# One fp32 chunk instead of three, x1's products and sum at other places, and one low part on VectorE

## What is computed

```python
e = jnp.stack([tbl_f[ids[:, f]] for f in range(39)], axis=1)      # 512 x 39 x 16
x0 = xk = e
for W in (f0, f1, f2):             # 39*39 x 128, 128*39 x 128, 128*39 x 128
    z = jnp.einsum('bfd,bgd->bfgd', x0, xk).reshape(b, f * g, d)
    xk = jnp.einsum('bpd,pm->bmd', z, W)
    outs.append(xk)
z = jnp.sum(jnp.concatenate(outs, axis=1), axis=-1)               # 512 x 384
h = jnp.concatenate([z, dense_ctx], axis=1)
h = jnp.maximum(h @ W_top1 + b_top1, 0.0)
h = jnp.maximum(h @ W_top2 + b_top2, 0.0)
y = h @ W_top3
```

## Time and profile before

| | before |
|---|---|
| median of 3 runs | 680.94 us (680.06 to 683.67) |
| profiled execution, its own time | 676.92 us |
| its span | 674.9 us |
| busy: PE, weight loads, DVE, ACT, POOL | 636.6, 504.6, 565.5, 374.1, 533.3 us |
| first bank of tiles 1, 2, 3, 4, 8 at | 83.9, 121.1, 158.4, 194.8, 348.3 us |
| last bank of the last tile ends at | 650.0 us |
| PE's granted clock | 0.995 of full speed |

### The profile page before, as it was taken

One profiled execution on the slowest core, in us unless ns is written; L12 is line 12 of the kernel. 1 busy time (PEld: TensorE's weight loads), 2 busy tenths in 40 slices (PEclk: granted clock), 3 DMA queues, 4 the chain that ended last, 5 costly groups with the idle time before them and its releaser, 6 DMA issues.

```text
span 674.9 us, 11454 instructions
## 1 busy us (share of the span) xinstructions
PE 636.6 (94%) x2900; PEld 504.6 (75%) x2900; DVE 565.5 (84%) x1934; ACT 374.1 (55%) x1129; POOL 533.3 (79%) x528
## 2 busy tenths in 40 slices
PE   3388999999999999999999999999999999999998
PEld 1256667777778788888878888888878888887867
DVE  4468888979899898989789898989879898988760
ACT  0445464646556574747467564746557474755431
POOL 6757879999999999998879999897969988574420
PEclk9999999999999999999999999999999999999989
DMA  9535642203241313113230322204031221200000
GB/s 185 112 70 140 211 117 68 62 6 89 40 110 18 98 29 81 44 29 95 43 85 8 84 44 66 60 10 113 10 88 37 63 62 41 81 0 1 2 0 1
DMA packets 79940, 42.25 MB, mean 63 GB/s; under 512 B 56721, under 2 KB 64721, under 8 KB 79746
## 3 DMA queue, kind: packets, MB, share of 16 engines
q1 hardware_dynamic: 67246, 35.85, 20.7%
q10 hardware_dynamic: 7380, 4.38, 3.2%
q0 software_dynamic: 5248, 1.29, 1.9%
HBM read 39.52 MB, written 1.94 MB: 61 GB/s over the span
## 4 chain that ended last, share of the span: by engine, by line
PE 68%; POOL 14%; DVE 5%; issue 5%; SPq 3%; ACT 2%; DMA 2%; POOLq 0%; DVEq 0%
PE y L900 16%; PE y L902 15%; PE y L901 15%; DVE scaled L802 4%; POOL emb_quads L481 4%; PE side L907 4%; PE late L918 4%; PE acc L882 3%; PE acc L877 3%; PE acc L876 3%; POOL sum L514 2%; POOL z_parts L499 2%; POOL sum L507 2%; ACT scaled L594 2%; PE y L918 2%
## 5 line engine op out<-in xcount | busy, mean ns | idle before, releaser
L802 DVE SCALAR_TENSOR_TENSOR scaled<-y,x_rows,scaled 128x128 f32<-128x128 f32 x1728 | 465.4, 341 | 63.4 <-ACT scaled L594 51.7
L594 ACT ACTIVATE scaled<-y,x_rows 128x128 f32<-128x128 f32 x768 | 218.9, 367 | 221.0 <-PE y L902 220.9
L900 PE MATMUL y<-w_hi,x_parts 128*128 128x512 f32 (+1 forms) x640 | 280.5, 438 | 9.5 <-DVE scaled L802 3.4
L902 PE MATMUL y<-w_hi,x_parts 128*128 128x512 f32 (+1 forms) x640 | 248.1, 388 | 0.0
L901 PE MATMUL y<-w_lo,x_parts 128*128 128x512 f32 (+1 forms) x640 | 247.6, 387 | 0.0
L481 POOL DMA_INDIRECT emb_quads<-in_small_tables_dram,quad_rows x144 | 139.2, 967 | 27.4 <-issue 15.6
L900 PEld LDWEIGHTS y<-w_hi,x_parts 128*128 128x128 f32 x640 | 120.6, 188 | 49.6 <-DVE scaled L802 23.0
L499 POOL TENSOR_TENSOR z_parts<-z,z_parts 117x512 fp32r<-117x512 f32 (+1 forms) x95 | 123.3, 1298 | 29.3 <-ACT z_parts L553 28.5
L902 PEld LDWEIGHTS y<-w_hi,x_parts 128*128 128x128 f32 x640 | 120.1, 188 | 24.9
L901 PEld LDWEIGHTS y<-w_lo,x_parts 128*128 128x128 f32 x640 | 121.0, 189 | 20.9 <-issue 2.6
L514 POOL TENSOR_TENSOR sum<-sum,scaled 128x512 f32<-128x512 f32 x63 | 81.7, 1296 | 26.5 <-DVE scaled L802 25.3
(11 more groups left out here) (94 smaller groups left out, 376.2 us busy)
## 6 DMA issues: line engine op xcount, KB each, us to landing
z<-x_turned SPq DMA_DIRECT2D x311, 78.0 KB
x_three<-x_turned SPq DMA_DIRECT2D x48, 78.0 KB
x_turned<-emb_quads SPq DMA_DIRECT2D x156, 8.0 KB
w_sb<-in_w_dram SPq DMA_DIRECT2D x1, 2496.0 KB, 9.6
emb_quads<-in_small_tables_dram,quad_rows POOLq DMA_INDIRECT x144, 2.4
s_sb<-in_w_dram ACTq DMA_DIRECT2D x12, 160.0 KB, 5.3
x_turned<-emb_singles SPq DMA_DIRECT2D x89, 2.0 KB
x_turned<-emb_quads SPq DMA_DIRECT2D x64, 2.0 KB
```

The costliest lines, as they stand in the source:

```text
L594: done = act.activation(scaled[:, k % 2, BY_ACT.index(j), i * M:(i + 1) * M], y2[n % RING][:, i * M:(i + 1) * M], ACT.Copy, scale=x0_rows[ ...
L802: dve.scalar_tensor_tensor(part, y2[n % RING][:, i * M:(i + 1) * M], x0_f, part, ALU.mult, ALU.add).then_inc(terms_in, 1)
L900: pe.matmul(dst, x1_hi[:, t % 2, cols], hi, start=True, stop=False)
L902: pe.matmul(dst, x1_lo[:, t % 2, cols], hi, start=False, stop=True).then_inc(y_ready, 1)
```

## The change

Five edits, which leave the arithmetic of each output the same but for the two chunks below:

- PLAIN is (3,) instead of (1, 3, 5): chunks 1 and 5 of tiles 1 to 4 take the way of the others (DVE's product, ACT's high part, POOL's low part, three fp32r matmuls).
- The low part of chunk 0 of each tile after the first is made by DVE at the place of the low part (slot 3), not by POOL.
- From tile 4 on (EARLY_FROM), DVE's products are at PRODUCTS_AT: chunks 0 and 1 at slots 28 and 32 of the tile before the one that they had, the others at 1, 6, 10, 15, 20. High parts, low parts and contractions keep their places.
- The sum of x1 is at slot 38 and not 36, and `rows` at slot 24 and not 30.
- From tile 4 on, gathers begin 24 slots ahead and not 14, and ACT copies x0 to PSUM at slot 26 and not 38.

```diff
@@
 GATHER_AHEAD = 14
+EARLY_AHEAD = 24
@@
-PLAIN = (1, 3, 5)
+PLAIN = (3,)
 PLAIN_TILES = range(1, 5)
@@
+EARLY_FROM = 4
+PRODUCTS_AT = (-12, -8, 1, 6, 10, 15, 20)
+SUM_AT = 38
 HIGH_LAG = 2
 LOW_LAG = 3
+
+DVE_LOW = 0
@@
-ROWS_AT = 30
+ROWS_AT = 24
 THREE_AT = 38
+EARLY_THREE_AT = 26
@@
+def product_at(t, s):
+
+    for u in (t + 1, t + 2):
+        places = FIRST_CHUNKS_AT if u == 1 else CHUNKS_AT if u < EARLY_FROM else PRODUCTS_AT
+        at = s - SLOTS * (u - 1 - t)
+        if u < TILES and at in places:
+            return u, places.index(at)
+    return None
+
+
+def three_at(u):
+    return EARLY_THREE_AT if u >= EARLY_FROM else THREE_AT
@@
 def low_by_dve(n):
-    return n in (0, 1, 3, 5, 6)
+    return n in (0, 1, 3, 5, 6) or n >= C0 and n % C0 == DVE_LOW
@@ gathers_at
-        first = (u - 2) * SLOTS - GATHER_AHEAD
+        first = (u - 2) * SLOTS - (EARLY_AHEAD if u >= EARLY_FROM else GATHER_AHEAD)
@@ POOL
-                    if c is not None and not plain(C0 * (t + 1) + c):
+                    if c is not None and not plain(C0 * (t + 1) + c) and not low_by_dve(C0 * (t + 1) + c):
                         low_part(t + 1, c)
@@ ACT
-                    if t + 2 < TILES and s == THREE_AT:
+                    if t + 2 < TILES and s == three_at(t + 2):
                         three(t + 2)
@@ DVE
-                    c = chunk_at(t + 1, s, 0)
-                    if c is not None and not plain(C0 * (t + 1) + c):
-                        product(t + 1, c)
+                    c = chunk_at(t + 1, s, LOW_LAG)
+                    if c is not None and low_by_dve(C0 * (t + 1) + c):
+                        low_part(t + 1, c)
+                    due = product_at(t, s)
+                    if due is not None and not plain(C0 * due[0] + due[1]):
+                        product(*due)
                     if t + 1 < TILES and s == ROWS_AT:
                         rows(t + 1)
                     if t + 1 < TILES and s == x1_at(t + 1) + 1:
                         x1_low(t + 1)
-                    if t + 1 < TILES and s == x1_at(t + 1) + 2:
+                    if t + 1 < TILES and s == SUM_AT:
                         sum_x1(t + 1)
```

15 lines of the change are left out of this document (8 added, 7 removed).

## The result

The changed kernel takes **686.72 us** (median of 18 runs, 684.04 to 690.78), the kernel before 680.73 in the same series of runs (18 runs, 678.19 to 684.31): ratio **1.0094**, 95% interval 1.0074 to 1.0114. So it is slower by 6.0 us, clear of the 0.5% that a measurement of this kernel can tell. The forecast was 683.5 and "no change", 3.2 us too low: the time lies inside the range of 675 to 690, but the change is not nothing.

What follows compares the result with a forecast made beforehand. PE was taken as the bound, losing some 11 us waiting for DVE and 3.3 for POOL. Terms 4.0 + 2.0 - 2.7 - 0.7 = +2.6 us gave 683.5 us against the 680.94 median; range 675 to 690.

Steps and rivals of the forecast that it cites:

- Respacing alone: nothing: DVE's burst: moving sum and products only shifts PE's stall from slots 1 and 2 to slot 3; 0 us.
- x0 fetched sooner: 0: ACT's copy of x0 at slot 26: the load is in by then, about 6.6 us against 6; 0 us.
- ACT must not wait for x0 at slot 26: Sign of being wrong: ACT waiting for x0 at slot 26; no size given.
- Gathers in tile 1: POOL has three more gathers between slots 19 and 26, so low parts of chunks 5 and 6 come late: +4.0 us.
- Rival 3: The jam goes on: POOL also late for chunks 3 to 6 in tiles 2 and 3, +3 us, 686.5; chance 0.12.
- DVE's added work, +2.0: DVE's extra low parts and products delay PE: 0.45 us each in tiles 4, 8, 12, 0.5 in 2, 0.2 in 3.
- POOL's waits gone, -2.7: From tile 2 on, PE's waits for POOL go, as POOL loses a low part a tile: -2.7 us.
- un-plained chunks, -0.7: On PE, three fp32r matmuls replace each plain chunk, saving 0.17 us each; those in tiles 0 and 1 bring nothing: -0.7 us.
- Rival 1: Banks of slots 37 and 38, freed sooner, let PE ahead and half of 11 us goes: 673; chance 0.14.
- Rival 2: At slot 3 DVE's low part waits for POOL's SBUF instruction, 9.8 us in all, 693; chance 0.14.
- a tile from 5 on that changes by over 0.6: Sign of being wrong: tiles 5 to 15 were each to stay within 0.5 us of before.

Runs made afterwards that it cites:

- b: The changed kernel with only the sum of x1 back at slot 36: 680.40 us, ratio 1.0036 to the kernel before.
- h: Changed kernel, old plain chunks, chunk 0's low part on POOL, sum at 36, x0's copy at 27, gathers earlier by two slots a tile, products from tile 8: ratio 1.0034.
- f: The changed kernel with the sum of x1 back at slot 36 and x0's copy at slot 27, not 26: 683.23 us, ratio 1.0038.
- g: The kernel before with only the gathers changed, 24 slots ahead for tiles from 4 on: 683.75 us, ratio 1.0042.
- d: The changed kernel with chunks 1, 3 and 5 plain again in tiles 1 to 4: 685.96 us, ratio 1.0123.
- a: The changed kernel with gathers, products and x0's copy at their old places in all tiles: 681.96 us, ratio 1.0070.
- c: The changed kernel with chunk 0's low part back on POOL in every tile: 681.50 us, ratio 1.0069.
- i: The kernel before, run again without any edit: 678.73 us, ratio 1.0021.
- j: The changed kernel, run again without any edit: 683.12 us, ratio 1.0083 to the kernel before.

## Why the prediction was wrong, point by point

- **"Respacing alone: nothing": the step that failed.** It measured +2.2 us (b). That the stall moves to slot 3 is right. But the text followed the bank of slot 39 behind "the same instructions as before" and took DVE to go on "without a pause". It did not ask whether ACT had evacuated bank 36, onto which DVE adds bank 37: with the sum gone from slot 36 DVE waits for ACT, 0.30 us at the end of tile 5, and work that filled a gap now adds to the burst. The rows that it read the earlier trace rows are of the end of tile 7, one of the five where ACT is done 0.77 us ahead and where the term is indeed nothing; at the end of nine other tiles it is 0.31 to 0.55. The other half of the term, two products in place of `rows` at slots 28 and 32, was right (b; h has the products so from tile 8 on).
- **"x0 fetched sooner: 0": failed too.** It asked only if the load is in and where the copy stands behind the evacuation, not what stands behind the copy. In tiles 7 and 11 that is the relu that PE waits for: +0.9 us (529.3 less 528.4, from b to f). The forecast's sentence that ACT must not wait for x0 at slot 26 held; that was not the danger.
- **"Gathers in tile 1": right.** +4.0 forecast, +3.6 and +4.2 measured, in two stalls of 2.2 and 1.6 us. The gathers alone make a jam as long (g), and beside them the un-plained chunk only divides it (d). But taking the early places back leaves 1.2 us (a: 38.49 against 37.29), 0.99 of them the un-plained chunk's stall, which the forecast counted in with the gathers. Rival 3, that POOL stays late in tiles 2 and 3, is out: they are 1.0 us shorter together.
- **DVE's added work, +2.0: right in place, the low part's share in size.** Tiles 4, 8 and 12 lose 0.44 us each on average by it (c), forecast 0.45. The rest of the term was not measured apart.
- **POOL's waits gone, -2.7, and un-plained chunks, -0.7: too much.** Tiles 2 and 3 gain 1.0 us. Tiles 2 to 15 should have gained 1.4 and lost 2.6; of these 4.0 us the two failed steps are 3.1, and the rest, some 0.9, is left by subtraction for this term and DVE's.
- **Rival 1 (the burst eases)** fell: PE's waits for DVE grew from 23.0 to 26.1 us, and slot 3 takes back what slot 1 gains. **Rival 2 (collision)** was to decide if DVE's low parts last over 1 us, and was out under 0.8. The loop's low parts in the page of the changed kernel (busy, mean ns):

```profile
L765 DVE TENSOR_TENSOR z_parts<-z,z_parts 117x512 fp32r<-117x512 f32 (+1 forms) x20 | 14.1, 707 | 0.1
```

- **Sum.** +2.6 us was forecast, and +6.0 us came between medians, 5.75 in the later series; in the tiles 1 to 15 it is 6.2 (572.4 less 566.2), and 6.5 in i and j. That the time lies in the range is luck, since the range was wide for the jam and DVE's work and not for the two terms put at 0. One of the prediction's own signs of being wrong, a tile from 5 on that changes by over 0.6, came true in tiles 7 and 11 (+0.7 and +0.8). Of the two profiled executions of the changed kernel, 684.04 and 679.97, the second is near the forecast's 679.5 by chance: beside it the kernel before had 675.43, 1.5 less than in the first profile.

## What to carry to other kernels

Moving work off a burst helps only if the engine has something else to do at once in the place it left: read in the timeline whether the next input is there by then, or the move turns hidden work into waiting. Ask of every moved instruction what stands behind it on its own engine in every kind of tile, the rare ones too, not only whether its input has come. And when work is shifted earlier by a fixed distance, one tile gets both schedules; look at that tile first, and when you spread the step out, check in each tile what now falls ahead of an instruction that the bottleneck is about to need.
